# A gated cross-attention and mixture-of-experts block on one core: 64-row score matmuls without partition transfers, float32 second matmuls for the first batch, head pairs normalised together

## What is computed

```python
q1 = x1 @ Wq1;  k = concat(x1 @ Wk1, x2 @ Wk2);  v = concat(x1 @ Wv1, x2 @ Wv2)   # 8 heads of 64
attn = softmax(q1 k^T * 64 ** -0.5)             # 256 queries, 768 keys
out = (attn @ v) @ Wo + bo
x = x + tanh(g_xattn[0]) * out                  # x1 = layernorm(x), x2 = ctx

logits = xf @ gate_w + gate_b                   # xf = layernorm(x)
top_w, top_i = top_k(logits, 2); gw = softmax(top_w)
for e in range(8):
    h = gelu(xf @ w1[e] + b1[e])                # 128 -> 512
    out = out + combine[:, e] * (h @ w2[e] + b2[e])
shared = gelu(xf @ ws1 + bs1) @ ws2 + bs2
x = x + tanh(g_ffn[0]) * (out + shared)
```

## Time and profile before

| | us |
|---|---|
| median of 3 runs | 173.5 (173.12 to 173.61) |
| the profiled execution's own time | 172.02 |
| its span, first to last instruction | 169.7 |

### The profile page before, as it was taken

The page is one execution under the profiler, slowest core; times in us unless marked ns, Lnnn a source line. Parts: engine busy times, 40 slices in busy tenths (PEclk is TensorE's granted clock), DMA queues, the critical chain, the costliest instruction groups (busy, mean ns, idle before and its releaser), DMA issues.

```text
span 169.7 us, 4332 instructions
## 1 busy us (share of the span) xinstructions
PE 139.7 (82%) x1724; PEld 111.5 (66%) x1724; DVE 131.2 (77%) x255; ACT 109.6 (65%) x182; POOL 126.8 (75%) x90
## 2 busy tenths in 40 slices
PE   7789588558699989999998892979866995999953
PEld 4435234335478768787787792869856994999952
DVE  1779999667667868768869689989999889454691
ACT  3369583329969979899968998569523462555600
POOL 7609999919999999989777955596557585868750
PEclk9999999999999999999999999999996999999999
DMA  4598699990004800995000000340000000100000
GB/s 136 184 315 211 196 238 242 220 251 14 6 0 85 198 1 16 217 233 191 4 4 0 4 0 0 108 144 6 2 0 0 4 0 4 31 0 4 0 0 31
DMA packets 12925, 13.99 MB, mean 82 GB/s; under 512 B 1470, under 2 KB 9579, under 8 KB 12907
## 3 DMA queue, kind: packets, MB, share of 16 engines
q1 hardware_dynamic: 12906, 13.73, 30.4%
HBM read 7.18 MB, written 0.26 MB: 44 GB/s over the span
## 4 chain that ended last, share of the span: by engine, by line
PE 32%; DVE 28%; POOL 10%; ACT 9%; DMA 8%; SPq 6%; issue 5%; DVEq 0%; ACTq 0%
PE banks L906 5%; DVE kab L852 5%; PE banks L908 5%; PE banks L907 5%; POOL kab L549 4%; ACT kab L642 4%; DVE v_lo L720 3%; DMA kab<-k_nat 3%; DVE nmax L735 3%; PE banks L1006 3%; PE banks L1007 3%; PE banks L987 3%; DMA ring<-in_L_ffn_w_dram 3%; SPq L425 2%; DVE gtop L763 2%
## 5 line engine op out<-in xcount | busy, mean ns | idle before, releaser
L549 POOL TENSOR_TENSOR kab<-kab 128x1024 f16<-128x1024 f32 (+1 forms) x18 | 41.1, 2283 | 17.3 <-DVE kab L852 17.3
L521 POOL TENSOR_TENSOR p_lo<-prob,p_hi 128x768 f16<-128x768 f32 x31 | 50.3, 1642 | 3.1 <-ACT p_hi L606 2.6
L642 ACT ACTIVATE kab<-banks,b1T 128x256 f32<-128x256 f32 x72 | 28.2, 478 | 24.3 <-PE banks L908 15.9
L735 DVE TENSOR_REDUCE nmax<-banks 128x1 f32<-128x768 f32 x32 | 30.5, 954 | 12.5 <-PE banks L988 12.5
L598 ACT ACTIVATE prob<-banks 128x768 f32<-128x768 f32 x32 | 25.8, 805 | 9.1 <-PE banks L1007 8.1
L906 PE MATMUL banks<-wf,kab 128*128 128x128 f16 x144 | 26.2, 224 | 5.8 <-POOL kab L549 4.5
L606 ACT ACTIVATE p_hi<-prob 128x768 f16<-128x768 f32 x32 | 27.0, 843 | 1.0
L852 DVE CAST kab<-kab 128x1024 f16<-128x1024 f32 (+1 forms) x19 | 19.5, 1031 | 9.8 <-ACT kab L642 9.8
L908 PE MATMUL banks<-wf,kab 128*128 128x128 f16 x144 | 26.2, 224 | 0.0
L907 PE MATMUL banks<-wf,kab 128*128 128x128 f16 x144 | 26.2, 224 | 0.0
L1006 PE MATMUL banks<-qab,kab 128*128 128x256 f16 x96 | 23.0, 273 | 0.7 <-DVE qab L832 0.7
(11 more groups left out here) (144 smaller groups left out, 340.3 us busy)
## 6 DMA issues: line engine op xcount, KB each, us to landing
ring<-in_L_ffn_w_dram SPq DMA_DIRECT2D x16, 256.0 KB, 4.1
kab<-k_nat SPq DMA_DIRECT2D x4, 384.0 KB, 4.4
kab<-k_nat SPq DMA_DIRECT2D x6, 192.0 KB, 4.4
kab<-k_nat SPq DMA_DIRECT2D x2, 576.0 KB, 7.2
qab<-qo SPq DMA_DIRECT2D x2, 384.0 KB, 6.2
kab<-k_nat SPq DMA_DIRECT2D x2, 288.0 KB, 7.8
prob<-in_ctx_dram SPq DMA_DIRECT2D x2, 256.0 KB, 5.4
ring<-in_L_xattn_Wk_dram SPq DMA_DIRECT2D x2, 256.0 KB, 3.9
```

Of the source, the lines that this page charges most:

```text
L521: nc.gpsimd.tensor_tensor(p_lo[:, j % 3, dst, :], prob(j, g)[:, 0:n, :], p_hi[:, j % 3, dst, :], ALU.subtract).then_inc(pl_done, 1)
L549: nc.gpsimd.tensor_tensor(hid_lo[:, k % HB, cols], hid[:, k % 2, cols], hid_hi[:, k % HB, cols], ALU.subtract).then_inc(hl_done, 1)
L642: nc.scalar.activation(hid[:, k % 2, c * T1:(c + 1) * T1], span(2 * (k % 2), HC * T1)[:, c * T1:(c + 1) * T1], ACT.Gelu, bias=b1T[:, e * H ...
L735: nc.vector.tensor_reduce(nmax[:, i, q:q + 1], span(0, KEYS), AX_X, ALU.max, negate=True).then_inc(max_done, 1)
```

## The change

- **Scores.** `kab`, `qab`, `stack_k`, `stack_q`, `k_st` and `q_st` are gone. `scores` reads keys and queries where the projection left them: a matmul has 64 rows, of partitions 0 to 63 for one head of the pair and 64 to 127 for the other, and the two heads' matmuls alternate, with their results in two banks. A key tile takes four matmuls a head: hi x hi, lo x hi, hi x lo and the shift, which has become a 64-row matmul of `ones_row` with `shift`. Work goes in 24 units of two key tiles, 256 queries and two heads (1024 columns), which share one pair of banks until unit 15 (`DOUBLE0`) and alternate between two pairs afterwards.
- **Maximum.** A pair's approximate scores come in three chunks: two of 512 context keys for 128 queries each (two heads), one of the 256 own keys for all queries. DVE reduces each chunk (`part_max`, 1024 columns) and then the parts (`whole_max`). The maximum, its transpose and its shift are made once a pair.
- **Order.** Four items run ahead (`PRE`), two between the first chunks, and 21 between the units (`LATE`, by step). `CHUNK0` = -4 and `FFN0` = 24. The stages of the tail have steps of their own (`TAIL_STEP`), and some of them use bank 6.
- **Normalising.** `reciprocals` and `normalise` take both heads of a pair at once.
- **Experts.** For the nine experts of the first batch and the last of the second (`FULL32`) the second product is one float32 matmul where there were three fp16 ones, straight from `hid` and the loaded weights; high and low halves of `hid` aren't made for them. For the other eight, ACT and DVE make half of the high half each. The weight ring has seven slots, `hid` three; a slot is loaded again when its float32 product is made (`y_ps`) and its second weights are split.
- **Splits.** ACT scales Wv2, Wv1 and Wo for POOL; early weights are split by POOL (high) and DVE (low), later ones by ACT, DVE and POOL in halves at fixed steps.
- **Small work.** Part of the gate's small operations moves from DVE to POOL and ACT; `bo` is added by a float32 matmul of one row; the output of the second batch is stored in two pieces.

The diff, cut to its core:

```diff
-ST_LAG = 2
-HI_LAG = 3
-PV_LAG = 4
-FFN0 = NH + ST_LAG
+KT2 = 2
+UPP = KT // KT2
+NPAIR = B * PAIRS
+NU = NPAIR * UPP
+RINGP = 7
+RINGE = 3
+CHUNK0 = -(UPP + 1)
+DOUBLE0 = 15
+FFN0 = NU
...
+TAIL_STEP = [dict(zip(TAIL_STAGES, (16, 17, 19, 22, 23, 28, 29))),
+             dict(zip(TAIL_STAGES, (27, 27, 28, 31, 32, 36, 37)))]
+COMB_STEP = [26, 35]
...
+def values_of(s):
+
+    if s >= NU + 1:
+        return NH - 2 + s - (NU + 1) if s <= NU + 2 else None
+    p, r = divmod(s - (UPP + 2), UPP)
+    return 2 * p + r if p >= 0 and r < 2 and p < NPAIR - 1 else None
...
+PRE = [(("tc", 0), 0), (("tx", 0), 2), (("k", 0, 0), 4), (("q", 0), 6)]
+LATE = {
+    -3: [(("k", 0, 1), 4)],
+    -2: [(("q", 1), 7)],
+    0: [(("k", 0, 2), 4), (("q", 2), 7)],
+    1: [(("v", 0, 0), 4), (("v", 0, 1), 5), (("v", 0, 2), 7)],
+    2: [(("v", 0, 3), 4), (("v", 0, 4), 5)],
+    3: [(("v", 0, 5), 7)],
+    4: [(("k", 0, 3), 4), (("q", 3), 7)],
+    5: [(("tc", 1), 7)],
+    6: [(("k", 1, 0), 4)],
+    7: [(("v", 1, 0), 4), (("v", 1, 1), 5), (("v", 1, 2), 7)],
+    8: [(("k", 1, 1), 4)],
+    9: [(("v", 1, 3), 7)],
+    10: [(("v", 1, 4), 4), (("v", 1, 5), 5)],
+    11: [(("k", 1, 2), 4)],
+    13: [(("k", 1, 3), 4)],
+}
...
-SHARED_LO = range(NF - 1, NF)
+NHID = 3
+
+FULL32 = [*range(NE), NF - 1]
...
-            def stack_k(b, p0, p1):
...
-                for half in range(2):
-                    src = slice(DH * half, DH * half + DH)
-                    heads = slice(place(2 * p0 + half), place(2 * p1 + half - 2) + 1)
-                    sp.dma_start(kab[0:DH, :, heads, :],
-                                 k_nat[src, 0:1, p0:p1, :].broadcast_to([DH, 2, p1 - p0, KEYS])).then_inc(done, 16)
...
+                elif j >= RING:
+                    sp.wait_ge(y_ps, j - RING + 1)
+                    if j > RING:
+                        sp.wait_ge(w2_lo, j - RING)
...
+            def exp_unit(u):
+
+                act.wait_ge(score_ps, u + 1)
+                if u >= RINGE:
+                    act.wait_ge(pl_done, u - RINGE + 1)
+                nc.scalar.activation(prob[:, u % RINGE, :], units(u).rearrange("p a n -> p (a n)"), ACT.Exp,
                                      scale=DH ** -0.5 / S_SCORE).then_inc(exp_done, 1)
...
+            def part_max(p, c):
+
+                dve.wait_ge(max_ps, UPP * p + c + 1)
+                if c < QT:
+                    first = max_bank(p, c)
+                    src, dst = banks[:, first:first + 2, :], part[:, p % 2, 0, :, c]
+                else:
+                    src, dst = banks[:, 0:2, :].rearrange("p h (q n) -> p h q n", q=QT), part[:, p % 2, 1, :, :]
+                nc.vector.tensor_reduce(dst, src, AX_X, ALU.max).then_inc(part_done, 1)
...
             def normalise(j):
                 b, h = divmod(j, HEADS)
                 settle()
-                nc.vector.tensor_tensor(o_sb[:, QT * b:QT * b + QT, h * DH:(h + 1) * DH], o_ps[:, :, 0:DH],
-                                        rsum[:, j, :].unsqueeze(2).broadcast_to([P, QT, DH]),
+                both = o_sb[:, QT * b:QT * b + QT, (h - 1) * DH:(h + 1) * DH].rearrange("p t (h d) -> p h t d", h=2)
+                nc.vector.tensor_tensor(both, o_ps[:, :, :, 0:DH],
+                                        rsum[:, j - 1:j + 1, :].unsqueeze(3).broadcast_to([P, 2, QT, DH]),
                                         ALU.mult).then_inc(o_done, 1)
...
+            def scores(u):
+
+                p, third = divmod(u, UPP)
...
+                tiles = [(n, half, slice(n * T1, (n + 1) * T1), slice((KT2 * third + n) * P, (KT2 * third + n + 1) * P))
+                         for n in range(KT2) for half in range(2)]
+                for n, half, cols, keys in tiles:
+                    nc.tensor.matmul(dst[:, half, cols], k_of(p, half, 0, keys), q_of(p, half, 0, every),
+                                     start=(n == 0), stop=False)
...
+                for n, half, cols, keys in tiles:
+                    nc.tensor.matmul(dst[:, half, cols], k_of(p, half, 1, keys), q_of(p, half, 0, every),
+                                     start=False, stop=False)
...
+                for n, half, cols, keys in tiles:
+                    nc.tensor.matmul(dst[:, half, cols], k_of(p, half, 0, keys), q_of(p, half, 1, every),
+                                     start=False, stop=False)
...
+                for n, half, cols, keys in tiles:
+                    rows = slice(DH * half, DH * half + DH)
+                    last = nc.tensor.matmul(dst[:, half, cols], ones_row[rows, :], shift[rows, p % 2, :],
+                                            start=False, stop=(n == KT2 - 1))
+                last.then_inc(score_ps, 1)
...
+            for i in range(CHUNK0, STEPS):
+                if 0 <= i < NU:
+                    scores(i)
...
+                if values_of(i) is not None:
+                    values(values_of(i))
+                if shift_of(i) is not None:
+                    shift_row(shift_of(i))
+                if chunk_of(i) is not None:
+                    max_chunk(*chunk_of(i))
+                for n in late_items(i):
+                    item_of(n)
...
+                            if k in FULL32:
+                                last = nc.tensor.matmul(banks[:, 4 + k % 2, q * D:(q + 1) * D],
+                                                        hid[:, k % NHID, at:at + P], ring_f(k % NE)[:, 1, cols],
+                                                        start=(c == 0), stop=(c == HC - 1))
+                                continue
```

More of the change, by code:

```diff
@@ L164, in hi_count @@
-def hi_count(k):
-    return k + shared(k)
-def hid_parts(k):
-    return [(0, HC // 2), (HC // 2, HC)] if k in SHARED_LO else [(0, HC)]
-def shifts_before(n):
-    return sum(1 for u, m in MISC.items() if m < n and u[0] == "shift")
+BIAS_STEP = 13
+EARLY = 4
+EARLY_HI_STEP = (14, 17, 20)
+EARLY_LO_STEP = (16, 19, 22)
+WO_STEP = 12
+W1_STEP = {4: FFN0, 5: FFN0 + 1, 6: FFN0 + 3, 7: FFN0 + 5, 8: FFN0 + 6}
+W2_STEP = {1: FFN0 + 2, 2: FFN0 + 4, 3: FFN0 + 7, 4: FFN0 + 8}
+W2P_STEP = {5: FFN0 + 4, 6: FFN0 + 5, 7: FFN0 + 6, 8: FFN0 + 8}
@@ new lines, with late_items, items_at, banks_of @@
+NI = len(ITEMS)
+WARM_START, WARM_LAYERNORM, WARM_MAX, WARM_STEP = 14, 9, 4, 12
+def late_items(s):
+    n = len(PRE) + sum(len(LATE[r]) for r in LATE if r < s)
+    return list(range(n, n + len(LATE.get(s, []))))
+def items_at(s):
+    if s >= 0:
+        return late_items(s - 1)
+    return [n for r in range(CHUNK0, 0) for n in late_items(r)] if s == -1 else []
+def banks_of(n):
+    return {BANK[n], BANK[n] + 1} if ITEMS[n][0] == "k" else {BANK[n]}
+def before(n, banks):
+    return max([m + 1 for m in range(n) if banks_of(m) & set(banks)], default=0)
@@ L189, in plan_misc, with same_bank_before @@
     return {u: n for n, u in enumerate(uses)}
 MISC = plan_misc()
+def same_bank_before(use):
+    return max([n + 1 for u, n in MISC.items() if n < MISC[use] and (u in IN_BANK6) == (use in IN_BANK6)], default=0)
 def block_kernel(nc, x, ctx_in, g_xattn, g_ffn, Wq1, Wk1, Wv1, Wk2, Wv2, Wo, bo,
@@ L306, in block_kernel @@
         item_hi, item_lo = sem("item_hi"), sem("item_lo")
[L307 to L308 removed]
         max_ps = sem("max_ps")
[L310 removed]
+        part_done = sem("part_done")
+        nmax_done = sem("nmax_done")
+        shift_ps = sem("shift_ps")
         shift_done = sem("shift_done")
@@ L361, in item_out @@
             kind = ITEMS[n][0]
-            return span(2 * SLOT[n], KEYS if kind == "k" else 512)
+            return span(BANK[n], KEYS) if kind == "k" else banks[:, BANK[n], :]
         block = stack.enter_context(nc.Block())
@@ L775, in tail @@
+                dve.wait_ge(gate_done, b + 1)
+                link(nc.vector.tensor_reduce(gsum[:, tiles], first[:, tiles, :], AX_X, ALU.add))
+                nc.vector.reciprocal(gtop[:, tiles, 0], gsum[:, tiles]).then_inc(gate_sum, 1)
             def tail(b, s):
@@ L1026, in values @@
[L1026 to L1045 removed]
+            keep_warm(WARM_MAX, 2)
```

903 lines of the change are left out of this document (460 added, 443 removed).

## The result

| | before | after |
|---|---|---|
| median of the runs side by side, us | 173.56 (173.12 to 174.38, 4 runs) | 158.72 (158.71 to 158.98, 4 runs) |
| ratio | | 0.914 (95% interval 0.911 to 0.918) |
| own time and span of the profiled execution, us | 172.02, 169.7 | 158.72, 156.9 |
| first exponential starts, us | 37.76 | 18.54 |
| last copy of the probabilities ends, us | 98.99 | 92.78 |

The changed kernel is faster by 8.6%. The three stages give 19.2 us at the start, lose 13.0 in attention (74.2 us from the first exponential to the last copy, against 61.2), and give 6.5 in the experts; with 0.1 at the end that is the 12.8 us of span. In short, the time went out of the wait before attention.

The account below looks back on a forecast made before the run. Transfers held the start, four engines in step attention, DVE then PE the experts. First exponential 18.5, attention 73 to 91.5, PE's end 152.8, plus 2.9 makes span 155.7, plus 3.8 makes 159.5 us; range 151 to 173.

Parts of the forecast that it names:

- the 3.8: Added to the forecast span: 2.3 us from span to own time, 1.5 more to the median of the runs.
- Part 1: Start: without transfers of keys and queries, the first exponential comes at 18.5 us, 19.3 earlier; bounds 17 and 21.
- Part 2: Attention stretch: ACT 67.7 us and PE 68 share the bound; stretch 73, last copy ends at 91.5, 7.5 gained.
- the lower bound: Score matmuls on PE: two 64-row halves run at once, 0.87 us a unit against 1.74 at the upper bound.
- factor of 1.08: Attention stretch before the change over its busiest engine's time; applied to ACT's 67.7 us it gave 73.
- rival 2: Attention in lockstep: each step waits for its slowest engine, stretch 80, time 166 us; 0.20 together with rival 3.
- free overlap: Attention stretch takes only 67.7 us, without stalls: time 152.5 us; chance 0.14.
- Part 3: Experts: PE becomes the bound, ending at 152.8 us, 61.3 after attention; float32 second matmuls cost PE 4.2 us more.
- Rival 1: Attention's 64-row matmuls run one after another on PE: stretch 95 instead of 73, time 182 us; chance 0.15.
- Rival 3: Experts' float32 matmuls take 0.16 us a piece: 8 us more, time 167 us; 0.20 together with rival 2.
- rival 5: Weights of late experts arrive late, one load of 4 us once: 163 us; included in the forecast's own range, 0.49.

Follow-up runs that it names:

- b3_same_rows: Changed kernel with all 64-row matmuls on rows 0 to 63, so pairs can't run side by side: 176.27 us, ratio 1.023 to the kernel before.
- b4_serial_look: Changed kernel with a unit's eight score matmuls of one head, then the eight of the other, traced at full clock: 165.68 us (one run).
- c3_act_more: Changed kernel with one more 128x256 copy on ACT in each unit, 24 in all: 161.38 us, ratio 0.939 to the kernel before.
- a2_fp16_first: Changed kernel with the first batch's second matmuls in fp16 again, second weights split a few steps earlier: 163.72 us, ratio 0.952 to the kernel before.
- c4_pool_more: Changed kernel with one more 128x128 addition on POOL behind each low half of the probabilities, 23 planned: 158.80 us, ratio 0.923 to the kernel before.
- b2_lo_steps: Changed kernel with three low-half casts of expert weights on DVE issued one step earlier: 157.91 us, ratio 0.916 to the kernel before.
- c2_hold_lo: Changed kernel with the edits of c1_hold and b2_lo_steps together: 157.71 us, ratio 0.918 to the kernel before.
- c1_hold: Changed kernel with PE's matmuls of the first batch's tail issued behind the next step's scores: 160.00 us, ratio 0.928 to the kernel before.

## Why the prediction was right, point by point

- **Forecast.** 159.5 predicted, 158.72 measured. The span was forecast at 155.7 and is 156.9; the 3.8 that I added to it was too much. The own time stands 1.8 above the span, not 2.3, and the median is that own time, not 1.5 above it. Two errors of 1 and 2 us stand against each other; that the time came within 0.8 is luck in that.
- **Part 1.** Key read-out kept at 10.53: 10.57. First exponential 18.5: 18.54. The three reductions took 3.49 (3.7). I had put the wait before down to the transfers alone, and the rows of the kernel before show two causes, one behind the other. The first pair's last transfer was issued at 17.50 and landed 2.1 later, at 19.6; the first approximate scores start at 22.96, behind the 18 items ahead in PE's order. The first scores (36.89) then stand behind the approximate scores of the next pair, which start at 36.57, when that pair's last transfer lands (issued at 30.64, 5.8 later 36.5). The change takes both away, the transfers and 14 of the 18 items, and no run has one without the other.

```profile
22.96 0.38 PE L987 MATMUL banks<-kab,qab 128*128 128x512 f16 x1
...
36.57 0.38 PE L987 MATMUL banks<-kab,qab 128*128 128x512 f16 x1 [1.70 <-issue]
...
36.89 0.27 PE L1006 MATMUL banks<-qab,kab 128*128 128x256 f16 x1
```

- **Part 2, ACT's and POOL's durations.** Exponential 1.02 (1.021), copy 1.08 (1.057), low half 2.15 (2.150), reduction 1.22 (1.214). Scaling by columns from a row of the same instruction held to about 2%. ACT's busy time was 63.5 where I summed 67.7. Its two large groups are 49.9 as summed (50.4); I had put the items and the tail too high, and neighbouring records overlap by a few hundredths each.
- **Part 2, PE.** A pair at 0.11, the lower bound, which I had taken for reasons and not from a row: shown by the pair's starts and by b3_same_rows. A change of arrangement costs 0.1 us each way (49.95 to 50.08 for 0.03, and 50.08 to 50.40 for 0.215), 0.2 there and back and not 0.3: 30 of them are 6 us, not 9. "TensorEngine Tiling (Array Packing)", section Key Properties, in the Trainium skill, has the switch draining the engine; the rows agree as far as they show a gap, and it is 0.1 us. Its other property, that tiles work independently, agrees with b4_serial_look, beyond what I had made of it: the second half starts while the first is five matmuls in. The estimate of 0.14 a pair that I had drawn from "TensorE: Matmul & The Clock Gate", section Part 3, in the Trainium skill, did not come; two 64-row tiles gave 1.76 / 0.88 = 2.0 times.
- **Part 2, the stretch.** 73 predicted, 74.2 measured, by the factor of 1.08 over ACT. The number was right and its reason only half. ACT is not the engine that the stretch follows: c3_act_more shows 0.35 us for each us more on ACT, b3_same_rows 0.62 and b4_serial_look 0.55 on PE. PE, which I had at 68 too, has 66.7 of the 73.5 us. The lockstep sum of rival 2 was 79.7; the truth lies between it (steps 0 to 13: 45.9 for 49.4; the rest: 28.3 for 30.3) and the 67.7 of free overlap. Of ACT's 9.9 us of idle time in the stretch 4.2 lie in two places, 71.7 to 76.3 and 78.7 to 83.1, where the first batch's tail, a cast and the next pair's shift row queue up on DVE and PE, and 4.3 are spread over steps 0 to 13.
- **Part 3.** Float32 second products: sixteen pieces, 0.112 apart, 1.79 us (1.76). PE without a gap from 92 us on, a period of 3.1 us where nothing else lies between (114.83 to 117.94; 3.3 to the next at 121.26), POOL at 10.6 of 31. PE from the last copy to its last matmul: 61.3 predicted, 61.3 measured. I had priced the float32 form as a cost of 4.2 us on PE against a gain of the other engines that I did not price; a2_fp16_first gives the sum of both, 4 to 5 us gained.
- **Rivals.** Rival 1 (b3_same_rows) did not come, and its kernel measured 176.3 where I gave 182. Rival 3 (0.16 a piece) and rival 5 (late weights: no wait for a weight load from 92 us on) did not come either.

## What to carry to other kernels

The order of transfers and of projections can hold a stage up for longer than either takes; ask which operation could start if the data never had to move and nothing stood ahead of it, here the 10.5 us read-out against the 37.8 us exponential. Two 64-row matmuls on different halves of the rows, with their results in different banks (one bank for both wasn't tried), count as one in PE's sum if they alternate in the order; eight and eight, half of the overlap is left. A change between 64 and 128 rows costs 0.1 us. Where two engines are busy beside each other and one of them slows down by it, moving work off both (here by float32 matmuls on PE) can gain more than it costs. One long distance in a periodic stage is worth looking at for all queues behind which it stands, since taking away the first can only uncover the next.

## What the runs showed of the hardware

- **DVE beside POOL.** DVE's cast of 128x512 with two inputs in memory (L925) takes 0.68 us alone and up to 2.55 while POOL makes p_lo, which is a difference of two tensors in memory. "SBUF — State Buffer", section Who interferes with whom, in the Trainium skill, says that a VectorE instruction with two SBUF inputs contends with a GpSimd instruction that reads SBUF; the traces agree. In attention casts 2.8 us shorter in sum came with a stretch 0.4 shorter (c4_pool_more, which adds work on POOL); moving them to other steps, still slowed (2.25, 1.98 and 1.23), gained 1.1 (b2_lo_steps). In the experts the slower casts are part of the 4 to 5 us of a2_fp16_first.
- **Row halves as queues.** PE starts the matmuls of the other half of the rows while three of the first half are still ahead in the order (47.04 in b4_serial_look, where the first half goes on to 47.36). Matmuls on different halves thus don't start in program order.
- **The clock.** The profiled execution of c2_hold_lo took 159.25 us at a mean granted clock of 0.987, where three others of it at 1.00 took 157.60 to 157.71. Its rows for PE (busy, clock) show the granted clock at its lower level, 1.2 GHz for 2.4, in most of the 4 us behind a stretch in which PE was busy 2.32 of 4:

```profile
88.00:92.00 4.00, 2.32 (x49) 1.00 0.02 4
92.00:96.00 4.00, 4.00 (x51) 0.57 0.00 0
```

In the changed kernel PE is busy 2.76 of the same 4 us, and its clock stays at 1.00. Why the clock falls in one execution and not in the next is open: c1_hold's profiled execution had 2.30 of 4 and kept its clock.
